# The second layer's edge lists, summed from bf16 halves by bf16 one-hot weights in the message bank

## The reference, cut to what matters

```python
h = maximum(layernorm(x), 0)
x = x + gat(h, adj, weight, att_weight)      # softmax over the neighbours of each row
h = maximum(layernorm(x), 0)
agg = adj @ h
msg = relu(agg @ W_msg.T + b_msg)
x = x + gru_cell(msg, h, W_ih, W_hh, b_ih, b_hh)
```

## Time and profile before

| what | value |
|---|---|
| median of 3 runs | 1273.13 us (1271.4 to 1283.29) |
| the profiled execution | 1273.98 us, its span 1272.2 us |
| adjacency halves | 128 of 2 MB |
| indirect DMAs on GpSimd | 480 |
| mean granted TensorE clock | 0.739 of full speed |

### The profile page before, as it was taken

The page is one execution under the profiler, slowest core; times in us unless marked ns, Lnnn a source line. Parts: engine busy times, 40 slices in busy tenths (PEclk is TensorE's granted clock), DMA queues, the critical chain, the costliest instruction groups (busy, mean ns, idle before and its releaser), DMA issues.

```text
span 1272.2 us, 12587 instructions
## 1 busy us (share of the span) xinstructions
PE 784.0 (62%) x3597; PEld 485.7 (38%) x3597; DVE 698.9 (55%) x2966; ACT 656.2 (52%) x662; POOL 500.9 (39%) x518
## 2 busy tenths in 40 slices
PE   2677548558584676858565656473835560079987
PEld 1444325234352443425332324241515540045644
DVE  7567537557384664847554546372737430057754
ACT  2767528558485764848564637372821410035532
POOL 3111543351624426153353534435343577710360
PEclk9887668776787767768675758585856675589998
DMA  9999949696796968769693939393710012200121
GB/s 323 421 418 424 411 142 404 262 405 279 283 387 259 413 250 357 322 256 416 258 408 142 411 134 416 125 407 121 323 26 13 23 51 53 52 22 30 54 72 34
DMA packets 55750, 305.52 MB, mean 240 GB/s; under 512 B 13825, under 2 KB 31442, under 8 KB 39296
## 3 DMA queue, kind: packets, MB, share of 16 engines
q1 hardware_dynamic: 27936, 274.74, 52.9%
q0 software_dynamic: 17152, 23.15, 6.9%
q10 hardware_dynamic: 10592, 6.82, 1.8%
HBM read 295.65 MB, written 12.71 MB: 242 GB/s over the span
## 4 chain that ended last, share of the span: by engine, by line
PE 27%; another core or an unknown queue 21%; DVE 17%; issue 17%; ACT 11%; DMA 5%; POOL 1%; ACTq 1%; DVEq 0%; POOLq 0%
PE ps L889 10%; ACT ind L636 9%; DVE cand L1329 3%; DMA x<-in_x 2%; PE ps L1090 2%; PE ps L981 1%; DMA adj_in<-in_adj 1%; PE ps L886 1%; PE ps L1112 1%; PE ps L1113 1%; POOL rows_in L522 1%; PE ps L927 1%; PE ps L1104 1%; PE ps L979 1%
## 5 line engine op out<-in xcount | busy, mean ns | idle before, releaser
L636 ACT ACTIVATE ind<-adj_in 128x4096 bf16<-128x4096 int32 x128 | 461.9, 3609 | 23.3 <-DMA adj_in<-in_adj 12.1
L889 PE MATMUL ps<-ind,bit_w 128*128 128x512 bf16 x1024 | 330.1, 469 | 76.5 <-ACT ind L636 50.5
L531 POOL DMA_INDIRECT val<-in_adj,val_idx x144 | 145.6, 1011 | 413.8 <-DVE val_idx L1521 346.9
L522 POOL DMA_INDIRECT rows_in<-wh_table,idx x192 | 193.1, 1006 | 99.0 <-issue 66.6
L889 PEld LDWEIGHTS ps<-ind,bit_w 128*128 128x128 bf16 x1024 | 116.1, 115 | 260.6 <-issue 129.7
L921 PE MATMUL ps<-pm,own 128*128 128x8 f32 x128 | 29.1, 356 | 187.9 <-issue 158.3
L587 POOL DMA_INDIRECT adj_in<-g_table,idx x96 | 92.9, 967 | 108.4 <-PE ps L1092 80.4
L921 PEld LDWEIGHTS ps<-pm,own 128*128 128x128 f32 x128 | 27.7, 319 | 194.9 <-issue 164.2
L1329 DVE MAX8 cand<-ps 128x8 f32<-128x256 f32 x256 | 90.7, 418 | 18.3 <-PE ps L889 16.4
L661 ACT COPY pm<-pm 128x32 f32<-128x32 f32 x16 | 3.5, 217 | 165.1 <-issue 123.4
L1635 DVE TENSOR_SCALAR adj_in<-iota,edge_row,val 128x128 f32<-128x128 f32 x128 | 34.4, 353 | 82.7 <-remote 81.0
(11 more groups left out here) (275 smaller groups left out, 1634.9 us busy)
## 6 DMA issues: line engine op xcount, KB each, us to landing
adj_in<-in_adj SPq DMA_DIRECT2D x128, 2048.0 KB
wh_table<-rows_in POOLq DMA_DIRECT2D x16, 264.0 KB, 8.5
g_table<-t_buf ACTq DMA_DIRECT2D x16, 256.0 KB
out<-rows_in SPq DMA_DIRECT2D x16, 256.0 KB
rows_in<-wh_table,idx POOLq DMA_INDIRECT x192
val<-in_adj,val_idx POOLq DMA_INDIRECT x144
adj_in<-g_table,idx POOLq DMA_INDIRECT x112
ind<-g_table,idx POOLq DMA_INDIRECT x16
```

Source lines behind the costliest of these rows:

```text
L522: nc.gpsimd.indirect_dma_start(out=rows_in[:, s % 2, t, k, :], out_offset=None, in_=wh_table, in_offset=bass.IndirectOffsetOnAxis(ap=idx[: ...
L531: nc.gpsimd.indirect_dma_start(out=val2[:, s, k:k + 1], out_offset=None, in_=adj_values, in_offset=bass.IndirectOffsetOnAxis(ap=val_idx2[: ...
L636: nc.scalar.activation(ind[:, (tile * 2 + half) % IND, :], adj_in[:, slot, 0:b - a].bitcast(I32), ACT.Relu, bias=1.0, scale=-1.0, accum_ou ...
L889: ins = nc.tensor.matmul(o, bit_w[:, b, :], ind[:, (tile * 2 + half) % IND, c0:c0 + HALF], start=False, stop=(b == BITS - 1))
```

## The change

The lists are multiplied in bf16. `after_off` holds only zeros and ones and becomes bf16, in half of its memory; the other half (`list_arena`) takes the bf16 halves of the differences and an f32 copy of the lists. `differences2` splits each difference into a bf16 value and the bf16 rest (`dsend_b`, `dover_b`), by two copies and two subtractions. The columns of a list matmul are the 21 first parts and the 21 rests, 42 columns, and the result has both sums beside each other, 9 x 42 numbers in bank 7 (bank 1 for the last two groups), which is also the bank of the messages `ps_tr`. `edges2` first adds the two by a reduce into `list2` in SBUF; what read PSUM in it now reads `list2`. `list2_read` is signalled by the instruction behind the reduce instead of the memset at the end. `send_lists2` no longer waits for `var2_done` (and `whbar_done`), but for `g_copied` of a group before; `message_columns` waits for `list2_read`.

```diff
-        after_off = sb("after_off", [P, 2, 2 * G, P])
+        list_arena = sb("list_arena", [P, 2 * 2 * G * P])
+        after_off = list_arena[:, 0:2 * G * P].bitcast(BF16).rearrange("p (h k r) -> p h k r", h=2, k=2 * G)
+        split = list_arena[:, 2 * G * P:2 * G * P + 2 * G * C2].bitcast(BF16).rearrange("p (a g x c) -> p a g x c", a=2, g=G, x=2)
+        dsend_b, dover_b = split[:, 0], split[:, 1]
+        list2 = list_arena[:, 3 * G * P:3 * G * P + E2 * C2].rearrange("p (e c) -> p e c", e=E2)
...
         def ps_list2(s):
-            return ps[:, 1 if s >= NG - 2 else 5, R0:R0 + E2 * C2].rearrange("p (e c) -> p e c", e=E2)
+            return ps[:, 1 if s >= NG - 2 else 7, 0:E2 * 2 * C2].rearrange("p (e x c) -> p e x c", e=E2, x=2)
...
                     if not isinstance(s, int) or s >= 1:
                         pe.wait_ge(g_copied, s)
+                    if s < NG - 3:
+                        pe.wait_ge(list2_read, s + 2)
...
                     if s == 0:
-                        pe.wait_ge(whbar_done, 1)
-                    elif s < NG - 2:
-                        pe.wait_ge(var2_done, s)
+                        pe.wait_ge(hT_done, NG)
+                    elif 2 <= s < NG - 2:
+                        pe.wait_ge(g_copied, s - 1)
                     for h in range(2):
                         for t in range(G):
-                            nc.tensor.matmul(ps_list2(s)[:, h * 5 + t, :], after_off[:, h, t, :], dsend[:, t, :], start=True, stop=True)
+                            nc.tensor.matmul(ps_list2(s)[:, h * 5 + t], after_off[:, h, t, :], dsend_b[:, t], start=True, stop=True)
                     for n in range(2 * G):
-                        ins = nc.tensor.matmul(ps_list2(s)[:, G, :], after_off[:, n // G, G + n % G, :],
-                                               dsend_over[:, n % G, :] if n else dsend[:, 0, :], start=(n == 0), stop=(n == 2 * G - 1))
+                        ins = nc.tensor.matmul(ps_list2(s)[:, G], after_off[:, n // G, G + n % G, :],
+                                               dover_b[:, n % G] if n else dsend_b[:, 0], start=(n == 0), stop=(n == 2 * G - 1))
...
                     V.tensor_tensor(dsend_over[:, 0, :], dsend[:, 0, :], wrapped[:, G - 1, :], ALU.subtract)
+                    link(V.tensor_copy(dsend_b[:, :, 0, :], dsend[:]))
+                    link(V.tensor_copy(dover_b[:, :, 0, :], dsend_over[:]))
+                    V.tensor_tensor(dsend_b[:, :, 1, :], dsend[:], dsend_b[:, :, 0, :], ALU.subtract)
+                    V.tensor_tensor(dover_b[:, :, 1, :], dsend_over[:], dover_b[:, :, 0, :], ALU.subtract)
...
                     dve.wait_ge(list2_mm, s + 1)
-                    V.tensor_scalar(place2[:, :, 0:G], ps_main2(s), -1.0, pid[:, 0:1], ALU.mult, ALU.add)
-                    link(V.tensor_scalar(place2[:, :, G], ps_list2(s)[:, G, K + 2:K + 4], -1.0, pid[:, 0:1], ALU.mult, ALU.add))
+                    link(V.tensor_reduce(list2[:], ps_list2(s).rearrange("p e x c -> p e c x"), AX.X, ALU.add))
+                    V.tensor_scalar(place2[:, :, 0:G], main2, -1.0, pid[:, 0:1], ALU.mult, ALU.add).then_inc(list2_read, 1)
+                    link(V.tensor_scalar(place2[:, :, G], list2[:, G, K + 2:K + 4], -1.0, pid[:, 0:1], ALU.mult, ALU.add))
...
-                    link(V.tensor_tensor(picked2, sel2, ps_list2(s)[:, :, 0:K], ALU.mult))
+                    link(V.tensor_tensor(picked2, sel2, list2[:, :, 0:K], ALU.mult))
...
-                    V.memset(unsure[:, s, :], 0.0).then_inc(list2_read, 1)
+                    V.memset(unsure[:, s, :], 0.0)
```

9 lines of the change are left out of this document (4 added, 5 removed).

## The result

| | changed | before, same measurement | ratio, 95% interval |
|---|---|---|---|
| 19 runs each | 1295.37 us (1286.9 to 1300.11) | 1281.4 us (1271.4 to 1286.95) | 1.0109 [1.0086, 1.0131] |
| profiled execution, span | 1289.81, 1288.0 us | 1273.98, 1272.2 us | |

The change costs 13.9 us (1.1%); 12.6 (1.0%) were forecast. The 1295.37 lie above the forecast's range all the same, mainly because the kernel before is at 1281.4 in 19 runs and not at the 1273.13 of three.

What follows compares the result with a forecast made beforehand. Bound: POOL's gather bursts alternating with Vector's stretch L1493 to L1521. 1.39 us, 13 times, is 18.1; minus 6.5 of waits leaves 11.6, plus 0.4 and 0.6 makes 12.6: 1285.7 us; range for 8 in 10, 1276 to 1292.

Steps and rivals of the forecast that it cites:

- The cycle of burst, release, stretch and issue: Period of a group: gathers 27.1 us, 2.9 until Vector starts, Vector's L1493 to L1521 23.6, 0.8 to POOL's next issue.
- The split, 0.80 us: In differences2 on Vector: two linked copies and two subtractions of 84 elements add 0.80 us per group, 0.70 to 0.95.
- The reduce, 545 ns and 0.59 linked: In edges2: a reduce of 378 PSUM elements to 189 adds 545 ns, 0.59 us with link and wake.
- the strided price of L1416: Other bound for the edges2 reduce: 806 ns, 0.85 us linked; 0.26 us more, 14 times, giving 1289.3 us.
- The bf16 output buys nothing: In differences2: L1498's two comparisons, now writing bf16, still take 2.35 us; halving would save some 1.07 us per group.
- Waits that vanish, 6.5 us: In the 13 stretches: 3.6 us at L1504 for lists and some 0.29 us each in nine others at a search go.
- The lists in bf16, 2.0 us a group: On TensorE: 17 loads and 17 matmuls take 2.0 us on the fast clock, twice that on the slow, against about 5.0.
- Both vanish under 0.80 us and faster lists: Step of the sum: Vector's waits for TensorE, 6.5 us, all go, leaving a balance of 11.6 of the 18.1 us added.
- The clock rival: The pack before a search stays at 1.2 GHz; each group pays 1.5 us, in half of them 10 us: 1296; chance 0.10.
- The ends: Outside the 13 stretches: 0.4 us before the first row gather and 0.6 for the last edges2's reduce.
- The level: Forecast time of 1285.7 us, 1.0% above the 1273.13 us taken for the kernel before.
- Not slower, because ScalarE covers it: Rival: ScalarE sets the search of 636.16, so the 0.80 us are covered: 1275; chance 0.16 with halved comparisons, 1271 to 1279.

Runs made afterwards that it cites:

- e1_split: Kernel before plus only the two copies and two subtractions in differences2, results unused, lists still f32 in bank 5; 1290.07 us, ratio 1.0131 to before.
- r3_changed: The changed kernel, unedited, timed again beside the kernel before, unedited; 1290.17 us, ratio 1.0099 to before.
- r1_changed: The changed kernel, unedited, timed again on an occasion where the kernel before took 1298.1 us; 1299.21 us, ratio 1.0016.
- D: Measurement with the kernel before at 1274.8 us; the unedited changed kernel took 1290.17 us there, ratio 1.0099.
- e4: Changed kernel with two unused f32 matmuls in front of the aggregate's wait; 1285.84 us, ratio 1.0101 to before; repeated, 1288.29 us, 1.0092.
- e11_bank_early: Kernel before with f32 lists in bank 7 and the after_off comparisons in front of Vector's wait for neighbours2; 1281.70 us, ratio 0.9932.
- B: Measurement with the kernel before at 975.3 us and four variants at 974.83 to 986.88 us; the changed kernel itself was not run there.
- e7_again: Changed kernel without its reduce, both bf16 halves summed in PSUM by 34 matmuls of 21 columns; 1302.53 us, ratio 1.0029 to before.

## Why the prediction was right or wrong

- *The cycle of burst, release, stretch and issue*: right. Bursts (408.2 and 407.7 us in sum), lags (45.8 and 46.6) and the 0.8 us behind a stretch stayed; the stretches grew.
- *The split, 0.80 us*: measured 0.80. *The reduce, 545 ns and 0.59 linked*: 546 and 0.58; the strided price of L1416 does not hold in PSUM. *The bf16 output buys nothing*: 1218 ns for one comparison, 1217 before. By this, the trace agrees with the Trainium skill, VectorE: DVE Perf Modes, What auto-detection actually checks: the doubled mode wants every tensor in 16 bits, and here only the output is.
- *Waits that vanish, 6.5 us*: right for the sum, since no list matmul is waited for and eight stretches are at 23.31 + 1.38. Their nature was wrong: e1_split shows that they go with TensorE's clock and that the split would have raised the ones for the lists to 8.2 us.
- *The lists in bf16, 2.0 us a group*: 0.6. A group has 16 list matmuls and not the 17 of the working (8 of L979, 8 of L981), which matters little; but the pitch of the f32 records was not the bf16 price, and "about half" became a sixth. It cost the forecast nothing, since nothing waits for them.
- *The failed step is the clock*, in the sum, at "Both vanish under 0.80 us and faster lists". I put the clock beside the forecast as a rival of chance 0.10, with 1.5 us in half of the groups, and looked for the cause in TensorE's idle time behind the lists ("the aggregation in front of it, unchanged, is what raised the clock"). It was a term of the sum: the aggregate waits for `weigh`, `weigh` stands behind the 0.80 us, and the aggregate itself lost its clock. It did so in five stretches, 4.2 us in sum, on record; 2.9 and 3.5 us in r3_changed and r1_changed. The forecast had 321.1 us for the 13 stretches; they took 325.1, and without the gap 320.9. The clock rival's own price, 1296, is next to the 1295.37 by luck: it put 10 us on the pack, where 4 were lost on the aggregate.
- *The ends*: the first stretch began 1.9 us later on record (1.1 in D) where 0.4 were put, and from the end of the last stretch to the end of the span the changed kernel was 1.9 us shorter, where the last reduce was to cost 0.6. So 12.6 + 4.0 + 1.5 + 0.2 - 2.5 = 15.8, the span's difference. The two end terms aren't shown to be the change's: the first stretch begins at 182.6 to 186.2 us in five traces of the changed kernel and e4, and the last part takes 362.4 to 367.7 us in them. The 19 runs say 13.9, so the forecast of 12.6 as a difference is close, with a missing 4 us and ends that offset part of it.
- *The level*: 1285.7 was 1273.13 + 12.6. The three runs happened to be low; in 19 the kernel before is at 1281.4, and the same difference from there gives 1294.0. These 8.3 us are the larger part of the 9.7 by which 1285.7 was short.
- *Not slower, because ScalarE covers it*: it did not happen, and the two chains are close. ScalarE and Vector are level in front of `exps`, which covers no addition but takes back most of the cuts tried (all of it in the stages of e11_bank_early that aren't late).
- *Not foreseen*: the chain under the burst as a second bound. On record it had 1 us or more to spare in every stage behind 21 gathers, so it cost nothing there.

## What to carry to other kernels

Where an engine is moved later, look at who waits for it with a fast clock: a pause of 0.8 us in front of a TensorE block cost 0.4 to 1.0 us in the five of 13 stages where the clock had not yet risen. An addition to a chain is paid wherever the chain is the longest, a cut only as far as the next chain allows, so look for what ends at the same time before pricing either. When a cycle waits for "the end of a burst plus a constant", find the chain that runs under the burst and its slack; a chain with slack on one occasion is the bound on the next. And before blaming the work for a late signal, compare when it ended with when it was seen.

## What the runs showed of the hardware

- The kernel before took 975, 1275, 1291 and 1298 us on different occasions. What sets it isn't known; two of the occasions (B, 975, and D, 1275) were on the chip with the same number.
- While GpSimd issued its indirect DMAs, Vector went on 5.8 to 9.8 us in the mean (before, changed, e7_again) behind the end of TensorE's `places2`, and began a stretch only 2.7 us or more behind the burst's end in before. In B the same two delays were mostly under 2.5 and 0.7 us.
- A copy of 84 elements from f32 to bf16 took 0.25 to 0.47 us on GpSimd by itself, 1.19 and 1.24 beside Vector's comparisons of 1024 elements (1.22 each), and 0.20 on Vector; a subtraction of as many 0.33 and 0.25. A gather issue that ran beside such comparisons took up to 2.03 us and not 1.00. The Trainium skill, Trainium Architecture — The Big Picture, The five engines, in one table, has GpSimd at half of Vector's speed for streaming work; these short instructions by themselves were 1.2 to 2.4 times slower.
- With the same pause of 0.78 us in front of it the aggregate ran at 2.4 GHz from its start where the granted clock rose before the pause's end, and at 1.2 for 8 pairs or more where it was 0.50 throughout (three and five times in one execution; in the five other stages the pause was 0.99 us or longer and the clock up already).
